# Last attention: the weighing of a head pair moved to right behind a slot's scores

## The chip, the cores and the metric

The kernel runs on one NeuronCore of a Trainium2 chip. The metric is the device time of one execution in microseconds (us), the median of several runs. The engines named below are TensorE (PE in the rows, PEld its weight loads), VectorE (DVE), ScalarE (ACT), GpSimd (POOL) and SyncE (SP). Each executes its own instructions in order and they wait for one another with semaphores.

## What is computed

The reference is a stack of four gated layers over x of 16 sequences x 256 tokens x 128 channels, all in 32 bit. Each layer normalises x, sends it through a mixer and through a feed-forward part, and adds mixer * silu(feed-forward) to x. The change touches only the mixer of the last layer, a causal attention with 16 heads of 64 channels:

```python
q = einsum('bpm,imh->bpih', x, W_Q) + b_Q      # the same for k and v
scores = einsum('bpih,bqih->bipq', q, k) / 8
scores = where(causal, scores, -100000.0)
attn = softmax(scores, axis=-1)
z = einsum('bpih,biqp->bqih', v, attn)
out = einsum('bqih,ihm->bqm', z, W_O) + b_O
```

## The kernel before, in words

The last attention is `layer3_attention`. Its unit of work is a slot m, which stands for one pair of heads of one sequence (the code calls a sequence a batch b): 16 x 8 = 128 slots, and a few more at the end in which the pipeline runs empty. There is no planner: each engine runs a loop over the slots, written out by hand, and the order of the calls in that loop is the order of its work.

On TensorE these steps exist:

- `scores(m)` (L3007, L3009): q times k of the pair, each head from its own 64 partitions (64*128 in the rows), into one of two buffers `ps`. It waits until the exponentials of slot m - 2 are done.
- `turn(m)` (L3019): six transposes of the scaled probabilities of pair m into the one buffer `pt`. It waits for GpSimd's scaling and for VectorE's copy of the previous transposes.
- `weigh(m)` (L3033, L3035): v times the turned probabilities, each head into its own 64 partitions of `pz` (128*64 in the rows).
- `job(...)`: a projection into the one buffer `px`. There are three kinds: "qk" makes q and k of one pair (L2988, L2989), "v" makes a quarter of v of a sequence (L2992), "out" applies W_O to a whole sequence (L2982, 32 matmuls). A job first waits until all jobs before it have been saved out of `px`.

`PLAN` sets which jobs go with which slot. Counted within eight slots, slots 6, 7, 0 and 1 have a qk job and then a v job; slots 2, 3 and 5 have a qk job; slot 4 has the out job of the sequence before and then a qk job. In the first sequence qk jobs crowd into slot 0, and the v jobs lie in slots 1 to 4.

TensorE's order within a slot before the change is: scores(m), first job, turn(m - 2), weigh(m - 3), remaining jobs.

The other engines follow the same slots. VectorE adds the mask to `ps` (L3173), takes the maxima (L3175, L3177), saves k of a qk job or the result of an out job out of `px` (L3120, L3122), takes the reciprocal of the sums of slot m - 1 (L3185) and copies `pt` of slot m - 2 to `turned` (L3191); in slots 3 to 17 it also has steps of the routing of the next part. Before saving k it waits for ScalarE's save of q of the same job. ScalarE saves q (L3064) and v (L3070) out of `px`, makes the exponentials (L3078, four per slot), and saves z out of `pz` (L3087). Its order is: save of the first job, exponentials of m, save of z of m - 3, save of the second job. GpSimd scales the exponentials with the reciprocals (L2963, L2964) and copies the next x (L2956). SyncE issues six loads of weights at the beginning and nothing later.

The line numbers of the loops are those of the code below.

Of the kernel before, what the change touches and what calls it, by code (L numbers as in the profile page):

```python
# [2893 lines left out]
def layer3_attention(nc, c, st, w, ready, fetch, fetched, spent, logits, gate_b, w_tok, spare):  # L2894
# [6 lines left out]
    ALL = NB * PAIRS  # L2901
# [8 lines left out]
    last = max(jobs) + 1  # L2910
# [4 lines left out]
    with ExitStack() as ctx:  # L2915
# [25 lines left out]
        with phase(nc, names, BATCH // NB, spent=spent) as (block, i, sems):  # L2941
            (bias_ready, x_ready, job_ready, job_saved, k_saved, scores_ready, masked, max_ready, exp_ready, recip_ready, prob_ready, turn_ready,
             turned_saved, z_ready, z_saved, logits_ready, chance_ready, choose_step) = sems
            SLOTS = max(ALL + 4, last)

            @block.sync
            def _(sp):
# [20 lines left out]
            @block.tensor  # L2968
            def _(pe):
                pe.wait_ge(*ready)  # L2970
                def job(what, b, n):

                    m = turn_of[what, b, n]
                    if by_act[m]:
                        pe.wait_ge(job_saved, by_act[m])
                    if by_dve[m]:
                        pe.wait_ge(k_saved, by_dve[m])
                    if what == "out":
                        pe.wait_ge(z_saved, PAIRS * (b + 1))
                        for t in range(2):  # L2980
                            for g in range(PAIRS):
                                ins = pe.matmul(px[:, t * P:(t + 1) * P], z[:, b % 2, g, t * P:(t + 1) * P], wo[:, g, :],  # L2982
                                                start=(g == 0), stop=(g == PAIRS - 1))
                    else:
                        pe.wait_ge(x_ready, b + 1)
                        x = xs[:, b % 2, :]
                    if what == "qk":
                        pe.matmul(px[:, 0:SEQ], wq[:, n, :], x, start=True, stop=True)  # L2988
                        ins = pe.matmul(px[:, SEQ:], wk[:, n, :], x, start=True, stop=True)  # L2989
                    if what == "v":  # L2990
                        t, half = n % 2, n // 2
                        ins = pe.matmul(px[:, :], x[:, t * P:(t + 1) * P], wv[:, half * HALF:(half + 1) * HALF],  # L2992
                                        start=True, stop=True)
                    ins.then_inc(job_ready, 1)

                def scores(m):

                    b, n = m // PAIRS, m % PAIRS
                    done = turn_of["qk", b, n] + 1
                    pe.wait_ge(job_saved, by_act[done])  # L3000
                    pe.wait_ge(k_saved, by_dve[done])
                    if m >= 2:
                        pe.wait_ge(exp_ready, 4 * (m - 1))
                    both = [(ps[m % 2][:, h, :], q[h * HD:(h + 1) * HD, b % 2, n, :], k[h * HD:(h + 1) * HD, b % 2, n, :])
                            for h in range(2)]
                    for out, qh, kh in both:
                        pe.matmul(out[:, 0:P], qh[:, 0:P], kh[:, 0:P], start=True, stop=True)  # L3007
                    for out, qh, kh in both:
                        ins = pe.matmul(out[:, P:3 * P], qh[:, P:], kh[:, :], start=True, stop=True)  # L3009
                    ins.then_inc(scores_ready, 1)  # L3010

                def turn(m):

                    pe.wait_ge(prob_ready, 2 * m + 2)
                    if m >= 1:
                        pe.wait_ge(turned_saved, m)
                    for h in range(2):
                        for j in range(3):
                            ins = pe.transpose(pt[:, h, j * P:(j + 1) * P], prob[:, m % 4, h, j * P:(j + 1) * P], c.ident[:, :])  # L3019
                    ins.then_inc(turn_ready, 1)  # L3020

                def weigh(m):

                    b, n = m // PAIRS, m % PAIRS
                    if n % 4 == 0:
                        pe.wait_ge(job_saved, by_act[turn_of["v", b, 2 * (n // 4) + 1] + 1])
                    if m >= 1:
                        pe.wait_ge(z_saved, m)
                    pe.wait_ge(turned_saved, m + 1)
                    both = [(pz[h * HD:(h + 1) * HD, :], slice((2 * n + h) * HD, (2 * n + h + 1) * HD), turned[:, m % 2, h, :])  # L3030
                            for h in range(2)]
                    for out, cols, pr in both:
                        pe.matmul(out[:, 0:SEQ], v[:, b % 2, 0, cols], pr[:, 0:SEQ], start=True, stop=False, skip_group_check=True)  # L3033
                    for out, cols, pr in both:
                        ins = pe.matmul(out[:, P:SEQ], v[:, b % 2, 1, cols], pr[:, SEQ:], start=False, stop=True,  # L3035
                                        skip_group_check=True)
                    ins.then_inc(z_ready, 1)

                for m in range(SLOTS):
                    now = jobs.get(m, [])  # L3040
                    if m == 0:
                        job(*now[0])
                        now = now[1:]
                    if m < ALL:
                        scores(m)
                    for j in now[0:1]:
                        job(*j)
                    if 0 <= m - 2 < ALL:
                        turn(m - 2)
                    if 0 <= m - 3 < ALL:  # L3050
                        weigh(m - 3)
                    for j in now[1:]:
                        job(*j)

            @block.scalar
            def _(act):
                load_table(act, c, ACT.Exp)
                act.wait_ge(bias_ready, 1)
                def save(what, b, n):
                    act.wait_ge(job_ready, turn_of[what, b, n] + 1)  # L3060
                    if what == "qk":
                        if b >= 2:
                            act.wait_ge(scores_ready, PAIRS * (b - 2) + n + 1)
                        act.activation(q[:, b % 2, n, :], px[:, 0:SEQ], ACT.Identity, bias=bq8[:, n:n + 1], scale=1 / 8)\  # L3064
                           .then_inc(job_saved, 1)
                    else:
                        t, half = n % 2, n // 2
                        if b >= 2:
                            act.wait_ge(z_ready, PAIRS * (b - 1))
                        act.activation(v[:, b % 2, t, half * HALF:(half + 1) * HALF], px[:, :], ACT.Copy).then_inc(job_saved, 1)  # L3070

                def exp(m):
                    act.wait_ge(max_ready, 2 * m + 2)
                    if m >= 4:
                        act.wait_ge(turn_ready, m - 3)
                    for h in range(2):
                        for t, cols in ((0, slice(0, P)), (1, slice(P, 3 * P))):
                            act.activation(prob[:, m % 4, h, cols], ps[m % 2][:, h, cols], ACT.Exp, bias=neg_max[:, m % 4, h, t:t + 1],  # L3078
                                           accum_out=total[:, m % 4, h, t:t + 1]).then_inc(exp_ready, 1)

                def save_z(g):
                    b, n = g // PAIRS, g % PAIRS
                    act.wait_ge(z_ready, g + 1)
                    if b >= 2 and n == 0:
                        act.wait_ge(job_ready, turn_of["out", b - 2, 0] + 1)

                    act.activation(z[:, b % 2, n, :], pz[:, 0:SEQ], ACT.Identity, bias=bv[:, n:n + 1]).then_inc(z_saved, 1)  # L3087

                for m in range(SLOTS):
                    now = jobs.get(m, [])  # L3090
                    if m == 0:
                        save(*now[0])
                        now = now[1:]
                    for j in now[0:1]:
                        if j[0] != "out":
                            save(*j)
                    if m < ALL:
                        exp(m)
                    if 0 <= m - 3 < ALL:
                        save_z(m - 3)  # L3100
                    for j in now[1:]:
                        if j[0] != "out":
                            save(*j)
                    if m == 4:
                        act.wait_ge(logits_ready, 1)
                        act.activation(chance[:, :, :], chance[:, :, :], ACT.Exp, scale=-1.0).then_inc(chance_ready, 1)

            @block.vector
            def _(dve):
# [53 lines left out]

                for m in range(SLOTS):
                    now = jobs.get(m, [])
# [258 lines left out]
```

## Time and profile before

| | |
|---|---|
| median of 3 runs | 2275.07 us (2269.94 to 2275.17) |
| span of the profiled execution | 2277.2 us |
| this attention, first scores to start of the next part | 1540 to 2123 us |
| granted clock, mean over the span | 0.934 |
| TensorE busy over the span | 2059.6 us (90%) |

The span is that of one execution under the profiler. It lies 2.1 us above the median of the timed runs. Busy time of TensorE counts matmuls whose ends are modelled, so distances between starts say more than durations.

### The profile page before, as it was taken

To read this page: it belongs to the slowest core of one execution; us is meant where nothing else is said; L and a number is where in the kernel's file an instruction comes from. 1 tells how busy PE (TensorE), PEld (TensorE's weight loads), DVE (VectorE), ACT (ScalarE), POOL (GpSimd) and SP (SyncE) were. 2 spreads that over 40 slices of the span, in tenths; PEclk is the share of its full clock that TensorE was granted. 3 is DMA by queue.
4 is the path that set the end of the run, shared out by engine and by line. 5 is a ranking of instruction groups with operands and counts; after the bars stand their busy time and mean duration, and the time that the engine had idled before them with its cause. 6 is when DMAs were issued, how large, how long until landed. Compare 5 with 4: busy or idle time off the path is not lost. (4 is left out here: it accounts for less than half of the span.)

```text
span 2277.2 us, 47255 instructions
## 1 busy us (share of the span) xinstructions
PE 2059.6 (90%) x18551; PEld 1392.9 (61%) x18551; DVE 1348.3 (59%) x3481; ACT 1049.2 (46%) x2520; POOL 631.5 (28%) x720
## 2 busy tenths in 40 slices
PE   4989999988879999698867897959999999999998
PEld 2546666657766677454555555655666666666565
DVE  2017777754555555456536884147877777677677
ACT  4235656642244454322234436345666666666222
POOL 3016930002210000103762015652333333333000
PEclk9989999998999999899986558988999999999999
DMA  2026030002110000241251013330000000000000
GB/s 62 19 29 29 2 39 2 2 5 65 18 55 1 1 1 1 69 140 22 39 138 39 2 28 114 48 87 25 1 1 1 1 1 1 1 1 1 6 15 19
DMA packets 118330, 64.44 MB, mean 28 GB/s; under 512 B 65848, under 2 KB 113248, under 8 KB 116960
## 3 DMA queue, kind: packets, MB, share of 16 engines
q1 hardware_dynamic: 106128, 52.37, 9.8%
q0 software_dynamic: 11264, 8.66, 2.7%
q8 instruction: 150, 2.46, 0.5%
q14 instruction: 68, 0.56, 0.1%
q10 hardware_dynamic: 720, 0.40, 0.1%
HBM read 37.54 MB, written 23.86 MB: 27 GB/s over the span
## 5 line engine op out<-in xcount | busy, mean ns | idle before, releaser
L3078 ACT ACTIVATE l_prob<-l_ps,l_neg_max 128x128 f32<-128x128 f32 (+1 forms) x512 | 208.6, 420 | 47.3 <-DVE l_neg_max L3177 42.5
L1658 ACT ACTIVATE l0a_prob<-l0a_pst 128x1024 f32<-128x1024 f32 x128 | 131.2, 1025 | 119.7 <-PE l0a_pst L1576 119.7
L2963 POOL TENSOR_TENSOR l_prob<-l_prob,l_total 128x256 f32<-128x256 f32 x128 | 78.6, 614 | 366.0 <-DVE l_total L3185 366.0
L1709 DVE TENSOR_REDUCE l0a_peak<-l0a_ps 128x4 f32<-128x1024 f32 x128 | 156.2, 1221 | 15.8 <-PE l0a_ps L1571 13.7
L1571 PE MATMUL l0a_ps<-l0a_k,l0a_q 32*128 32x256 f32 x1024 | 146.3, 405 | 3.3 <-ACT l0a_prob L1658 2.5
L680 ACT ACTIVATE l0e_hidden<-l0e_ph,l0f_b 128x512 f32<-128x512 f32 x128 | 87.9, 687 | 129.2 <-PE l0e_ph L591 129.2
L1576 PE MATMUL l0a_pst<-l0a_q,l0a_k 32*128 32x256 f32 x1024 | 145.8, 400 | 0.2 <-ACT l0a_prob L1658 0.2
L3173 DVE TENSOR_TENSOR l_ps<-l_ps,future 128x512 f32<-128x512 f32 x128 | 89.4, 699 | 93.2 <-PE l_ps L3009 93.0
L601 PEld LDWEIGHTS l0e_py<-l0f_w,l0e_hidden 128*128 128x128 f32 x1024 | 119.7, 192 | 35.0 <-ACT l0e_hidden L680 32.6
L2964 POOL TENSOR_TENSOR l_prob<-l_prob,l_total 128x512 f32<-128x512 f32 x128 | 133.2, 1041 | 0.0
L601 PE MATMUL l0e_py<-l0f_w,l0e_hidden 128*128 128x128 f32 x1024 | 129.8, 280 | 0.3 <-ACT l0e_hidden L680 0.3
L3064 ACT ACTIVATE l_q<-l_px,l_bq 128x256 f32<-128x256 f32 x128 | 60.7, 474 | 144.1 <-PE l_px L2989 144.1
L591 PE MATMUL l0e_ph<-l0f_h_ch,l0f_w 128*128 128x512 f32 x256 | 123.3, 596 | 2.9 <-ACT l0e_hidden L680 1.8
L3191 DVE COPY l_prob_t<-l_pt 128x768 f32<-128x768 f32 x128 | 119.2, 931 | 4.0 <-PE l_pt L3019 1.8
L1571 PEld LDWEIGHTS l0a_ps<-l0a_k,l0a_q 32*128 32x128 f32 x1024 | 91.5, 187 | 30.5 <-issue 22.6
L3019 PE MATMUL l_pt<-ident,l_prob 128*128 128x128 f32 x768 | 105.0, 273 | 2.9 <-POOL l_prob L2964 2.6
L3078 ACT ACTIVATION_READ_ACCUMULATOR l_prob<-l_ps,l_neg_max 128x1 f32 x512 | 104.1, 203 | 0.0
L709 DVE SCALAR_TENSOR_TENSOR l0e_acc<-l0e_py,l0e_w,l0e_acc 128x128 f32<-128x128 f32 x192 | 54.1, 344 | 83.0 <-PE l0e_py L601 82.8
L3019 PEld LDWEIGHTS l_pt<-ident,l_prob 128*128 128x128 f32 x768 | 91.1, 141 | 15.3 <-POOL l_prob L2964 4.4
L2988 PE MATMUL l_px<-l_x,l_wq 128*128 128x256 f32 x256 | 91.1, 438 | 10.1 <-issue 5.6
L1576 PEld LDWEIGHTS l0a_pst<-l0a_q,l0a_k 32*128 32x128 f32 x1024 | 89.9, 184 | 1.5 <-issue 1.2
L1285 POOL TENSOR_TENSOR gr_k_in<-gr_k_tok,gd_k_scale 128x512 f32<-128x512 f32 x8 | 8.6, 1078 | 283.3 <-ACT gr_v_tok L1177 283.2
(533 smaller groups left out, 4936.4 us busy)
## 6 DMA issues: line engine op xcount, KB each, us to landing
l_band<-zero SPq DMA_DIRECT2D x16, 272.0 KB, 7.3
x_tok<-in_x_dram SPq DMA_DIRECT2D x2, 2048.0 KB, 8.3
l2f_w<-in_L_ffn_w_dram SPq DMA_DIRECT2D x2, 2048.0 KB, 10.0
l_rows<-l_band SPq DMA_DIRECT2D x16, 256.0 KB
l1f_w<-in_L_ffn_W_dram SPq DMA_DIRECT2D x3, 1024.0 KB, 11.3
gd_tri<-gp_tri SPq DMA_DIRECT2D x8, 256.0 KB, 2.0
l0f_w<-gd_tri SPq DMA_DIRECT2D x8, 256.0 KB, 11.5
gd_tri<-l0f_w SPq DMA_DIRECT2D x8, 256.0 KB, 8.4
```

What stands on the lines that cost most here:

```text
L591: pe.matmul(ph1[u % 2][:, :], w1[:, unit, :], x, start=True, stop=True).then_inc(h1_ready, 1)
L601: ins = pe.matmul(py[x % 2][:, j, :], hidden[:, x % 2, f, j * P:(j + 1) * P], w2[:, (x % n_exp) * chunks + f, :], start=(f == 0), stop=(f ...
L1571: ins = pe.matmul(ps[m % 2][:, j, t, :], left, right, start=True, stop=True)
L1576: ins = pe.matmul(pst[:, j, t, :], left, right, start=True, stop=True)
L1658: act.activation(prob[:, (n // 2) % 2, pair, :, :].rearrange("p g t s -> p g (t s)"), pst[:, :, :, :].rearrange("p g t s -> p g (t s)"), A ...
L1709: dve.tensor_reduce(to, ps[m % 2][:, :, :, :], AX.X, ALU.max, negate=True).then_inc(max_ready, 1)
L2964: pool.tensor_tensor(far, far, total[:, m % 4, :, 1:2].to_broadcast([P, 2, 2 * P]), ALU.mult).then_inc(prob_ready, 1)
L2988: pe.matmul(px[:, 0:SEQ], wq[:, n, :], x, start=True, stop=True)
L3019: ins = pe.transpose(pt[:, h, j * P:(j + 1) * P], prob[:, m % 4, h, j * P:(j + 1) * P], c.ident[:, :])
L3078: act.activation(prob[:, m % 4, h, cols], ps[m % 2][:, h, cols], ACT.Exp, bias=neg_max[:, m % 4, h, t:t + 1], accum_out=total[:, m % 4, h, ...
L3173: dve.tensor_tensor(diag, diag, future, ALU.add).then_inc(masked, 1)
L3191: dve.tensor_copy(turned[:, n % 2, :, :], pt[:, :, 0:3 * P]).then_inc(turned_saved, 1)
```

## The change

The weighing of a pair happens one slot later, and at another place in the slot: directly behind the scores, ahead of the first job. The order on TensorE becomes scores(m), weigh(m - 4), first job, turn(m - 2), remaining jobs. ScalarE's save of z moves with it, to the beginning of its slot. The number of slots is bounded by the pipeline's depth plus one; it stays 133, since the last out job already lies in slot 132. VectorE's, GpSimd's and SyncE's loops are as before.

```diff
-            SLOTS = max(ALL + 4, last)
+            SLOTS = max(ALL + 5, last)
...
             @block.tensor
...
                     if m < ALL:
                         scores(m)
+                    if 0 <= m - 4 < ALL:
+                        weigh(m - 4)
                     for j in now[0:1]:
                         job(*j)
                     if 0 <= m - 2 < ALL:
                         turn(m - 2)
-                    if 0 <= m - 3 < ALL:
-                        weigh(m - 3)
                     for j in now[1:]:
                         job(*j)
...
             @block.scalar
...
+                    if 0 <= m - 4 < ALL:
+                        save_z(m - 4)
                     for j in now[0:1]:
                         if j[0] != "out":
                             save(*j)
                     if m < ALL:
                         exp(m)
-                    if 0 <= m - 3 < ALL:
-                        save_z(m - 3)
                     for j in now[1:]:
                         if j[0] != "out":
                             save(*j)
```

## Rows read from the trace of the kernel before

**Rows 1.** Busy time per engine in one stretch: engines' us, granted clock, DMA share.

```profile
core 0: us, PE busy (x) PEld busy (x) DVE busy (x) ACT busy (x) POOL busy (x), PEclk, DMA share, GB/s
...
1600.00:2100.00 500.00, 493.15 (x3483) 335.93 (x3481) 357.49 (x696) 316.55 (x1182) 185.82 (x239) 1.00 0.01 1
```

**Rows 2.** Timeline of TensorE over one batch: start, us, engine, line, tiles.

```profile
1819.98 0.49 PE L3007 MATMUL l_ps<-l_k,l_q 64*128 64x128 f32 x4
...
1827.88 1.12 PE L2992 MATMUL l_px<-l_wv,l_x 128*128 128x512 f32 x2
1828.94 0.49 PE L3007 MATMUL l_ps<-l_k,l_q 64*128 64x128 f32 x4
...
1837.90 0.49 PE L3007 MATMUL l_ps<-l_k,l_q 64*128 64x128 f32 x4
...
1838.76 0.70 PE L2988 MATMUL l_px<-l_x,l_wq 128*128 128x256 f32 x2
1839.30 0.59 PE L2989 MATMUL l_px<-l_x,l_wk 128*128 128x256 f32 x2
1839.73 0.82 PE L3019 MATMUL l_pt<-ident,l_prob 128*128 128x128 f32 x6
1840.48 0.65 PE L3033 MATMUL l_pz<-l_prob_t,l_v 128*64 128x256 f32 x4
...
1841.28 0.49 PE L3007 MATMUL l_ps<-l_k,l_q 64*128 64x128 f32 x4
...
1843.10 0.82 PE L3019 MATMUL l_pt<-ident,l_prob 128*128 128x128 f32 x6
...
1849.18 0.82 PE L3019 MATMUL l_pt<-ident,l_prob 128*128 128x128 f32 x6
...
1851.27 0.59 PE L2989 MATMUL l_px<-l_x,l_wk 128*128 128x256 f32 x2
1851.79 0.49 PE L3007 MATMUL l_ps<-l_k,l_q 64*128 64x128 f32 x4
...
1853.09 0.67 PE L2988 MATMUL l_px<-l_x,l_wq 128*128 128x256 f32 x2 [0.38 <-issue]
...
1855.58 0.49 PE L3007 MATMUL l_ps<-l_k,l_q 64*128 64x128 f32 x4
```

**Rows 3.** Timeline of TensorE in the first layer's attention, 32-row to 32-column blocks.

```profile
398.83 0.37 PE L1576 MATMUL l0a_pst<-l0a_q,l0a_k 32*128 32x256 f32 x1
399.14 1.07 PE L1604 MATMUL l0a_pz<-l0a_prob,l0a_v 128*32 128x256 f32 x16
```

**Rows 4.** Timeline of all engines in the third slot of the last attention.

```profile
1554.16 0.59 PE L2989 MATMUL l_px<-l_x,l_wk 128*128 128x256 f32 x2
...
1554.59 0.82 PE L3019 MATMUL l_pt<-ident,l_prob 128*128 128x128 f32 x6
1554.79 0.47 ACT L3064 ACTIVATE l_q<-l_px,l_bq 128x256 f32<-128x256 f32 x1 [1.32 <-PE l_px L2989]
...
1555.41 0.47 DVE L3120 TENSOR_SCALAR l_k<-l_px,l_bk 128x256 f32<-128x256 f32 x1
...
1555.99 1.10 PE L2992 MATMUL l_px<-l_wv,l_x 128*128 128x512 f32 x2 [0.58 <-issue]
...
1557.01 0.38 PE L3007 MATMUL l_ps<-l_k,l_q 64*128 64x128 f32 x2
```

**Rows 5.** Timelines of VectorE and of GpSimd within the batch of rows 2.

```profile
1843.33 0.68 DVE L3177 TENSOR_REDUCE l_neg_max<-l_ps 128x2 f32<-128x512 f32 x1
...
1845.62 0.70 DVE L3173 TENSOR_TENSOR l_ps<-l_ps,future 128x512 f32<-128x512 f32 x1 [0.30 <-PE l_ps L3009]
...
1849.38 0.42 DVE L3122 TENSOR_TENSOR mixer_out<-l_px,l_bo 128x256 f32<-128x256 f32 x1 [2.00 <-PE l_px L2982]
...
1841.76 1.04 POOL L2964 TENSOR_TENSOR l_prob<-l_prob,l_total 128x512 f32<-128x512 f32 x1
```

**Rows 6.** Timeline of TensorE, where slots 4 and 22 start.

```profile
1561.44 0.49 PE L3007 MATMUL l_ps<-l_k,l_q 64*128 64x128 f32 x4
...
1641.96 0.49 PE L3007 MATMUL l_ps<-l_k,l_q 64*128 64x128 f32 x4
```

## The prediction

> **What bounds the kernel now.** I read the views in this order. First the busy time by stage: in 500 us of this attention TensorE is busy 493, VectorE 357, ScalarE 317, GpSimd 186, and the granted clock is 1.00, the 2.4 GHz level [rows 1]. So the stage is TensorE's, and the question is what fills it. Second TensorE's timeline of one batch of eight slots [rows 2]. The reader is to look there at the distance from one start to the next, not at the durations, because the durations overlap. The batch takes 1855.58 - 1819.98 = 35.60 us. Its four slots with a q/k job and a v job take (1837.90 - 1819.98)/4 = 4.48 on the average (I call them v slots); a slot with a q/k job alone takes 3.38 (1837.90 to 1841.28); the slot with the output job takes 7.14 (it starts another 3.37 after 1841.28, at 1844.65, and ends at 1851.79); the one after it takes 3.79, because its q/k job starts 1.82 us after the previous q/k job's second half (1851.27 to 1853.09).
>
> **The hidden price: changes of shape.** In [rows 2] the second half of a q/k job (two passes of 256 columns) takes 0.43 us with a block of the same 128*128 shape before and behind it (1839.30 to 1839.73). The first half is the same work and takes 0.54, as it comes behind the 64-row scores. So a block that begins with a change of shape pays 0.10 more. Ahead of the scores the second half takes 0.52 (1851.27 to 1851.79), so a block that ends in a change pays 0.09 more. The weighing (128*64) streams as many columns per head as the scores, and takes 0.80 (1840.48 to 1841.28) against 0.86 (1837.90 to 1838.76); I take its beginning as 0.05. Prices of one change, end and beginning together: scores to job 0.19, transposes to weighing 0.14, weighing to scores 0.19, weighing to job 0.19, job to scores 0.19; job to transposes and back costs nothing.
>
> **The change on TensorE.** No matmul is added or removed, only the order differs, and no DMA issue, SP or GpSimd instruction moves. The 0.80 us of weighing goes from behind the transposes to ahead of the job.
> - A slot with one job: before scores | job, transposes | weighing | (three changes); after scores | weighing | job, transposes | (three). By the blocks: 0.86 + 0.80 + 0.97 + 0.75 = 3.38 both ways. Scores to weighing does not occur in this stage. The nearest rows are those of the first layer's attention, where 32-row matmuls are followed by 128*32 ones: the last step is 399.14 - 398.83 = 0.31 [rows 3], where one pass of 256 columns takes 0.21 (half of 0.43). So it ends at 0.10, and I take 0.14 in all, like transposes to weighing. From below it could be nothing, from above 0.19; over 128 slots that is -18 to +6 us round my value.
> - A slot with two jobs: before four changes (0.19 + 0.14 + 0.19 + 0.19 = 0.71), after three (0.14 + 0.19 + 0.19 = 0.52). With everything ready a v slot would take 0.86 + 0.80 + 0.97 + 0.66 + 0.96 = 4.25: six transposes without a change behind them (0.75 - 0.09) and a v job without one ahead (1.06, from 1827.88 to 1828.94, less 0.10).
>
> **The wait that comes in.** All jobs write one bank, px. The second job's first matmul waits until ScalarE has saved q and VectorE, which waits for that save, has saved k. Before, transposes and weighing (0.75 + 0.80) lie between the q/k job and the v job; after, only the transposes. The trace already holds this very order: in the third slot (1554 us) there is nothing to weigh yet, and transposes are followed at once by the v job [rows 4]. q/k's second half starts at 1554.16, ScalarE's save of q at 1554.79, VectorE's save of k at 1555.41, over at 1555.88, and the v job at 1555.99: 1.83 after 1554.16, the same distance as the 1.82 of [rows 2]. Unhindered it would be 0.43 + 0.66 = 1.09. The wait is 0.74. Then the v job takes 1.02 (1555.99 to 1557.01) rather than 0.96, since its weights were not loaded ahead. A v slot after the change: 0.86 + 0.80 + 0.97 + 1.40 (1554.59 to 1555.99) + 1.02 = 5.05, against 4.48: +0.57.
>
> Could another engine make it later or earlier? VectorE's maxima end 2.73 behind the slot's start (1843.33 + 0.68 - 1841.28 [rows 2, 5]); after the change q/k's second half starts at 0.86 + 0.80 + 0.54 = 2.20 and the k save at 2.20 + 1.25 = 3.45, so VectorE stands waiting. ScalarE's step that now comes first, the save of z, can start when the weighing ends at 1.66 and is as short as q's (0.47); q's save starts at 2.20 + 0.63 = 2.83. Both saves are bound to the job's end alone, and nothing shortens them.
>
> **What follows from the shift elsewhere.** In one-job slots the k save, the reciprocal, GpSimd's scaling and the transposes that wait for it all shift by the same 0.80; scaling now ends at 1841.76 + 1.04 = 1842.80 and the transposes start at 1843.10 [rows 2, 5], so a slack of 0.30 stays. VectorE now needs 1.31 us from the end of the maxima (1844.01) through k save, reciprocal and copy of the transposed block, until it idles 0.30 before the mask at 1845.62 [rows 5]. With the k save at 3.45 these would end at about 3.45 + 1.31 + 0.1 = 4.86 behind the slot's start, where the next mask wants to begin at 3.38 + 0.97 = 4.35 (1845.62 less the slot's start at 1844.65): 0.5 late. But the maxima then end at 2.73 + 0.5 = 3.2 of their slot and the next k save is not due before 3.45, so the lateness does not add up.
> - Slot with the output job: after its last pass (0.11 before 1849.18) VectorE saves at 1849.38 for 0.42 [rows 2, 5], plus 0.10 until TensorE: 1849.90, which is 0.72 behind the transposes' start where 0.66 would do. In place of -0.19 I take -0.06 (bounds -0.19 and 0).
> - The slot behind it: the weighing now lies between the two q/k jobs and covers the wait: 3.79 becomes 3.38, -0.41.
>
> **The sum.** v slots from slot 4 on: one in the first batch and four in each of 15: 61 x 0.57 = +34.8. Some starting waits, where VectorE also does the routing, go under in the longer slots: slots 4 to 21 take 1641.96 - 1561.44 = 80.52 [rows 6], and the steady pattern would give 9 x 4.48 + 5 x 3.38 + 2 x (7.14 + 3.79) = 79.1: -1.4. Output slots 15 x -0.06 = -0.9. The slots behind them 15 x -0.41 = -6.2. Slot 3 loses its weighing and gets the wait: -0.2. In the tail TensorE waits for others, and one more weighing fits in there: 0, at most +-1. Together +26 us. The profiled span is 2277.2, 2 us above the median of 2275.1 and inside what runs differ by; I add to the median: **2301 us**.
>
> **A rule for the change and one against it.** The rows show 0.14 to 0.19 us per change of shape [rows 2]; this mechanism by itself is the rival "switches" below. The Trainium skill, TensorEngine Tiling (Array Packing), "Key Properties", says that changing the tiling mode, not merely the tile, drains the engine; by that rule alone the change is a gain. The rows also show px emptied 1.72 us behind the start of q/k's second half (1555.88 - 1554.16 [rows 4]). The same page of the Trainium skill, "PSUM Bottleneck", warns that tiling hastens TensorE and not the emptying of PSUM; by it the change only moves the wait, and the trace agrees.
>
> **Rivals.**
> - *Switches*: the px wait is hidden after all. Then 76 slots with two jobs save 0.19 (-14.4), and the waits behind the output job go (-6.2): 2254 us, faster. For it: the prices of changes are plain in [rows 2]. Against: [rows 4] shows transposes to v job at 1.40. It decides below a wait of about 0.3 us, for which the k save would have to come 0.45 earlier, as if it did not follow q's.
> - *The loop slips too*: the 0.30 of slack behind GpSimd is eaten, and the transposes wait about 0.2 in most slots: 128 x 0.2 = +26 more, 2327 us. Against it, all its links shift alike.
> - *Nothing*: scores to weighing costs nothing (-18), and the wait is 0.15 us shorter than [rows 4] show (61 x 0.15 = -9): 2301 - 27 = 2274 us.
>
> **How the numbers follow.** Forecast 0.84, switches 0.06, slipping loop 0.07, nothing 0.03. The forecast's own bounds are 2301 - 18 and 2301 + 6 from the unseen change, and some 6 us for starts that come later than in [rows 4]; the range is 2284 to 2315. What this kernel's measurement can tell from no change is 0.3%, about 7 us: faster 0.06, same 0.03, slower 0.91.
>
> **What would show it.** Right: v slots at 5.0 to 5.1 us, an idle time of about 0.6 ahead of each L2992 group released by the k save (some 35 us in all, where now there is none), 3.38 in one-job slots, and no idle ahead of L2988. Wrong: v slots near 4.24 (switches), one-job slots over 3.5 with idle ahead of L3019 (slipping loop), or one-job slots well off 3.38 with no idle (the unseen change).

## The result and the profile after

The changed kernel takes 2304.65 us (median, 2298.46 to 2306.24) against 2272.51 us for the kernel before, run beside it: a ratio of 1.0134, 95% interval 1.011 to 1.0159. That is +30 us (25 to 36), where +26 was forecast (2301, range 2284 to 2315). Its profiled span is 2302.6 us against 2277.2.

TensorE's timeline of one sequence after the change; it answers to [rows 2].

```profile
1831.10 0.49 PE L3007 MATMUL l_ps<-l_k,l_q 64*128 64x128 f32 x4
1831.43 0.60 PE L3009 MATMUL l_ps<-l_k,l_q 64*128 64x256 f32 x4
1831.96 0.65 PE L3033 MATMUL l_pz<-l_prob_t,l_v 128*64 128x256 f32 x4
1832.44 0.39 PE L3035 MATMUL l_pz<-l_prob_t,l_v 128*64 128x128 f32 x4
1832.76 0.70 PE L2988 MATMUL l_px<-l_x,l_wq 128*128 128x256 f32 x2
1833.30 0.59 PE L2989 MATMUL l_px<-l_x,l_wk 128*128 128x256 f32 x2
1833.73 0.82 PE L3019 MATMUL l_pt<-ident,l_prob 128*128 128x128 f32 x6
1835.12 1.10 PE L2992 MATMUL l_px<-l_wv,l_x 128*128 128x512 f32 x2 [0.58 <-issue]
1836.15 0.49 PE L3007 MATMUL l_ps<-l_k,l_q 64*128 64x128 f32 x4
...
1851.29 0.49 PE L3007 MATMUL l_ps<-l_k,l_q 64*128 64x128 f32 x4
...
1854.66 0.49 PE L3007 MATMUL l_ps<-l_k,l_q 64*128 64x128 f32 x4
...
1858.03 0.49 PE L3007 MATMUL l_ps<-l_k,l_q 64*128 64x128 f32 x4
...
1863.37 0.82 PE L3019 MATMUL l_pt<-ident,l_prob 128*128 128x128 f32 x6
1864.09 0.67 PE L2988 MATMUL l_px<-l_x,l_wq 128*128 128x256 f32 x2
1864.60 0.59 PE L2989 MATMUL l_px<-l_x,l_wk 128*128 128x256 f32 x2
1865.12 0.49 PE L3007 MATMUL l_ps<-l_k,l_q 64*128 64x128 f32 x4
...
1868.49 0.49 PE L3007 MATMUL l_ps<-l_k,l_q 64*128 64x128 f32 x4
```

The v slot takes 1836.15 - 1831.10 = 5.05 us, and 1.39 of it lie between the start of the transposes and the v job (1833.73 to 1835.12). The one-job slot takes 3.37 (1851.29 to 1854.66), the slot with the output job 7.09 (1858.03 to 1865.12), the one behind it 3.37 (to 1868.49), where it was 3.79. A sequence takes 1868.49 - 1831.10 = 37.39, against 35.60 in [rows 2].

What TensorE's own instructions waited for, from 1600 to 2100 us (total, times, longest). It is the only line; in the kernel before this stretch had 5.4 us ahead of L2988 and 0.4 ahead of L2992. The view names no releaser ("issue"), but the times of the two saves below do.

```profile
PE l_px L2992 <- issue: 30.9, 53, 0.9
```

The chain in that v slot on ScalarE and VectorE: save of q, save of k, then the v job above. It answers to [rows 4].

```profile
1833.93 0.47 ACT L3064 ACTIVATE l_q<-l_px,l_bq 128x256 f32<-128x256 f32 x1 [0.58 <-PE l_px L2989]
1834.54 0.48 DVE L3120 TENSOR_SCALAR l_k<-l_px,l_bk 128x256 f32<-128x256 f32 x1 [0.30 <-ACT l_q L3064]
```

The save of k ends at 1834.54 + 0.48 = 1835.02, the v job starts at 1835.12. VectorE had nothing to do for 0.30 before it, and the releaser is ScalarE's save.

### The profile page after: what moved, and what is told of

The parts are those of the page before. It is cut to its first block and busy times, and to the rows that moved or that the text cites. A ratio compares the mean times of both kernels' runs of the same rounds, so it can differ in the third digit from the quotient of the medians.

```text
span 2302.6 us, 47255 instructions
## 1 busy us (share of the span) xinstructions
PE 2068.1 (90%) x18551; PEld 1397.4 (61%) x18551; DVE 1349.6 (59%) x3481; ACT 1056.5 (46%) x2520; POOL 631.4 (27%) x720
## 5 line engine op out<-in xcount | busy, mean ns | idle before, releaser
L3120 DVE TENSOR_SCALAR l_k<-l_px,l_bk 128x256 f32<-128x256 f32 x128 | 61.9, 483 | 76.9 <-ACT l_q L3064 76.8
L3087 ACT ACTIVATE ffn_out<-l_pz,l_bv 128x256 f32<-128x256 f32 x128 | 60.8, 475 | 98.3 <-PE l_pz L3035 98.2
L2992 PE MATMUL l_px<-l_wv,l_x 128*128 128x512 f32 x128 | 71.1, 637 | 38.1 <-issue 36.9
## 6 DMA issues: line engine op xcount, KB each, us to landing
l0f_w<-gd_tri SPq DMA_DIRECT2D x8, 256.0 KB, 12.7
```

## The experiments

Each ratio is against runs of the kernel before on the same chip. The chips differ from one experiment to another, so the ratios are to be compared and not the medians. "Sequence" is the distance between the starts of slots 62 and 70 in the trace, the eight slots of one sequence in the steady part, in us.

| kernel | sequence | less before, x 15 | ratio, 95% interval |
|---|---|---|---|
| before | 35.60 | | |
| changed | 37.39 | +27 | 1.0134 (1.011 to 1.0159) |
| v job first | 35.33 | -4 | 0.9991 (0.9969 to 1.0014) |
| TensorE's part alone | 40.72 | +77 | 1.0333 (1.0289 to 1.0376) |
| k saved later | 38.73 | +47 | 1.0217 (1.0175 to 1.0259) |
| z saved early, old order | 35.39 | -3 | 0.9984 (0.9963 to 1.0004) |
| two orders | 35.62 | 0 | 1.0013 (0.9997 to 1.0029) |
| two orders, z behind v | 35.53 | -1 | 1.0002 (0.9983 to 1.0021) |
| one more change of shape | 35.92 | +5 | 1.0059 (1.0038 to 1.0081) |
| the same, reciprocals early | 35.08 | -8 | 0.9973 (0.9954 to 0.9992) |

(The last row is the kernel with two orders and z behind v, with early reciprocals.)

**The v job ahead of the q/k job.**

```diff
+    for t in jobs:
+        if t:
+            jobs[t].sort(key=lambda job: job[0] != "v")
```

> The changed kernel, but in slots with a q/k job and a v job the v job goes first. TensorE's changes of shape per slot stay three. Theory (the wait on px decides): the second job now waits for ScalarE's one save of v (starts 0.64 behind v's last pass, 0.62 long, 0.10 to TensorE), and no longer for two saves in a row; the wait falls from 0.74 to about 0.26 us, v slots from 5.05 to 4.57, 61 of them: 29 us less than the changed kernel, about 2275, level with the kernel before. Rival (the new order costs elsewhere, px is innocent): v slots stay at 5.05 and the time at 2304.

Measured 2273.33 us, ratio 0.9991 where the changed kernel has 1.0134: its whole loss is gone (a sequence is 2.06 us shorter, 31 us in 15; 29 was expected). A v slot of it, TensorE and ScalarE (three lines are inserted above, so numbers are 3 higher: L2995 is the v job, L3022 the transposes, L2991 and L2992 the q/k job, L3073 the save of v):

```profile
1849.92 1.13 PE L2995 MATMUL l_px<-l_wv,l_x 128*128 128x512 f32 x2
1850.88 0.82 PE L3022 MATMUL l_pt<-ident,l_prob 128*128 128x128 f32 x6
1851.08 0.60 ACT L3073 ACTIVATE l_v<-l_px 128x512 f32<-128x512 f32 x1 [0.57 <-PE l_px L2995]
1851.73 0.70 PE L2991 MATMUL l_px<-l_x,l_wq 128*128 128x256 f32 x2
```

The second job starts 0.85 behind the transposes instead of 1.39, right behind ScalarE's save. The slot takes 4.53. It has three changes of shape as the changed kernel has, and the weighing stands where the changed kernel has it, so the loss is the wait for px and not the weighing's place by itself. The saves of q and k now lie behind the slot's other work on ScalarE and VectorE too; scores and weighing of the next slot cover them.

**TensorE's part of the change alone.**

```diff
-                    if 0 <= m - 4 < ALL:
-                        save_z(m - 4)
                     for j in now[0:1]:
...
                     if m < ALL:
                         exp(m)
+                    if 0 <= m - 4 < ALL:
+                        save_z(m - 4)
```

> The changed kernel with ScalarE's save of z back at its old place, behind the exponentials; TensorE's order stays the new one. Theory: z of a pair is then saved about 5.4 us behind its slot's start, the next weighing wants pz at 3.37 + 0.86 = 4.23, so each slot behind a one-job slot (slots 2, 3 and 5 of eight) waits 1.3 us ahead of L3033, and these slots go from 3.37 to 4.67; v slots at 5.05 cover it. 45 such slots: +58 us, about 2362. Rival (the place of z's save is free, as ScalarE is only half busy): same as the changed kernel, 2304.

Measured 2350.59 us, ratio 1.0333. The weighing waits for ScalarE, which is nearly half idle (busy 267 of 500 us) but has z's save behind four exponentials:

```profile
1804.52 0.49 ACT L3087 ACTIVATE ffn_out<-l_pz,l_bv 128x256 f32<-128x256 f32 x1
1805.07 0.65 PE L3033 MATMUL l_pz<-l_prob_t,l_v 128*64 128x256 f32 x4 [1.02 <-ACT ffn_out L3087]
```

The places were as expected (slots 3, 4 and 6 of eight), the size a little less: 4.47, 8.23 and 6.14 in place of 3.37, 7.09 and 5.05, so 1.1 each and not 1.3, and 2351 in place of 2362. ScalarE's half of the diff is therefore needed, not decoration.

**The save of k made later.**

```diff
+                        if b and n < 4:
+                            dve.tensor_reduce(dummy[:, 4 * b + n:4 * b + n + 1], px[:, SEQ:], AX.X, ALU.max)
                         dve.tensor_scalar(k[:, b % 2, n, :], px[:, SEQ:], ...).then_inc(k_saved, 1)
```

> The changed kernel with one more VectorE reduction of 256 columns out of px ahead of the save of k in the 60 slots of sequences 1 to 15 that have a v job too; its result is not used. Theory (the serial saves of q and k set the v job): VectorE's start-to-start for such a reduction is 0.34 us, all of it goes to the wait, v slots 5.05 to 5.39: +20 us, about 2325. Rival (TensorE's v job waits for something else, its weights or ScalarE): the reduction falls into VectorE's idle time and costs under 3 us.

Measured 2324.56 us, ratio 1.0217. VectorE and the v job (line numbers are 1 to 3 higher):

```profile
1855.12 0.42 DVE L3122 TENSOR_REDUCE l_dummy<-l_px 128x1 f32<-128x256 f32 x1 [0.71 <-ACT l_q L3065]
1855.46 0.47 DVE L3123 TENSOR_SCALAR l_k<-l_px,l_bk 128x256 f32<-128x256 f32 x1
1856.03 1.10 PE L2993 MATMUL l_px<-l_wv,l_x 128*128 128x512 f32 x2 [0.91 <-issue]
```

The reduction delays the save by 0.34, and TensorE's idle time goes from 0.58 to 0.91: v slots take 5.38 instead of 5.05. The v job follows the save of k one for one: 19 us more than the changed kernel by the two ratios, where 20 were expected.

**ScalarE's part alone, TensorE's order as before.**

```diff
+                    if 0 <= m - 4 < ALL:
+                        save_z(m - 4)
                     for j in now[0:1]:
...
                     if m < ALL:
                         exp(m)
-                    if 0 <= m - 3 < ALL:
-                        save_z(m - 3)
```

> The kernel before with TensorE's order untouched; only ScalarE's save of z goes to the beginning of the next slot. Theory: in the kernel before every second v slot takes 4.53 in place of 4.43, because z's save stands ahead of v's and px is released 0.1 us late for the next q/k job. With z out of the way these fall to 4.43: 30 x 0.1 = 3 us less than before, about 2270. Rival (the 4.53 is TensorE's own): same as before within 1 us. If z came too late for the weighing it would show as idle time ahead of L3033.

Measured 2272.29 us, ratio 0.9984 (0.9963 to 1.0004). The runs alone don't settle 3 us, the trace does: all v slots take 4.43, as these three starts show, where every second one took 4.53.

```profile
1814.08 0.49 PE L3007 MATMUL l_ps<-l_k,l_q 64*128 64x128 f32 x4
...
1818.51 0.49 PE L3007 MATMUL l_ps<-l_k,l_q 64*128 64x128 f32 x4
...
1822.94 0.49 PE L3007 MATMUL l_ps<-l_k,l_q 64*128 64x128 f32 x4
```

**One more change of shape, cover untouched.**

```diff
+                    if 0 <= m - 3 < ALL:
+                        weigh(m - 3)
                     if 0 <= m - 2 < ALL:
                         turn(m - 2)
-                    if 0 <= m - 3 < ALL:
-                        weigh(m - 3)
```

> The kernel before with the weighing ahead of the transposes instead of behind them, both still between the first and the second job. The cover of px is the same 1.5 us. In one-job slots the changes of shape go from three to four (scores, job, weighing, transposes, scores); in slots with two jobs they stay four. Theory (a change costs 0.19 us by itself): slots 2, 3 and 5 of eight get 0.19 longer, v slots keep their length: 45 x 0.19 = 9 us more than before, about 2281. Rival (the prices read from the starts belong to the matmuls and not to the change): same as before.

Measured 2284.8 us, ratio 1.0059 (1.0038 to 1.0081). A one-job slot of it:

```profile
1842.60 0.49 PE L3007 MATMUL l_ps<-l_k,l_q 64*128 64x128 f32 x4
...
1843.46 0.70 PE L2988 MATMUL l_px<-l_x,l_wq 128*128 128x256 f32 x2
1843.99 0.59 PE L2989 MATMUL l_px<-l_x,l_wk 128*128 128x256 f32 x2
1844.52 0.65 PE L3033 MATMUL l_pz<-l_prob_t,l_v 128*64 128x256 f32 x4
1845.00 0.39 PE L3035 MATMUL l_pz<-l_prob_t,l_v 128*64 128x128 f32 x4
1845.32 0.87 PE L3019 MATMUL l_pt<-ident,l_prob 128*128 128x128 f32 x6
1846.12 0.49 PE L3007 MATMUL l_ps<-l_k,l_q 64*128 64x128 f32 x4
```

The slot takes 3.52 and not 3.37, with no idle time: the fourth change costs 0.15, not 0.19. The transposes take 0.80 between two changes against 0.75 with one [rows 2], so their beginning costs 0.05, half of a projection's 0.10. V slots became 0.05 shorter in half of the cases (4.38), for the same reason; the steady slots' sum gives +5 us, and the runs +9 to +18. The trace shows 1.8 us more at the end: from the last scores to the next part it takes 17.13 us and not 15.35, as the weighing, now ahead of the transposes, waits there for the saves of z and for VectorE's copies (1.1 to 1.2 us each time). Slots 4 to 126 grew by 5.2 us in all. Slots 0 to 3 took another 2.8 us, at the lower clock, as in the changed kernel (see below). So a change has a price of its own, and the rival is out; what the runs show beyond these 7 us stays open.

A v slot of the same run shows the v job behind the transposes with no wait between them:

```profile
1823.96 0.87 PE L3019 MATMUL l_pt<-ident,l_prob 128*128 128x128 f32 x6
1824.67 1.02 PE L2992 MATMUL l_px<-l_wv,l_x 128*128 128x512 f32 x2
1825.63 0.49 PE L3007 MATMUL l_ps<-l_k,l_q 64*128 64x128 f32 x4
```

**Two orders: the new one only where no v job follows.**

```diff
+                    late = any(j[0] == "v" for j in now)
-                    if 0 <= m - 4 < ALL:
+                    if 0 <= m - 4 < ALL and not late:
                         weigh(m - 4)
...
                         turn(m - 2)
+                    if 0 <= m - 4 < ALL and late:
+                        weigh(m - 4)
```

(ScalarE's save of z likewise: first in its slot, or behind the exponentials. The second kernel, "z behind v", also has ScalarE save v before z in those v slots that another v slot follows.)

> The changed kernel with two orders: in slots without a v job the new one, in slots with a v job the weighing (and z's save) behind the transposes as before, so that it lies between the q/k job and the v job again. Theory (px wait loses, everything else of the change gains): v slots return to 4.43 to 4.54, the slot of the output job stays at 7.09 and the one behind it at 3.37, instead of 7.14 and 3.79; per sequence 0.47 less than before: 7 us less than before, about 2267. Rival (the mixed order brings a new wait for z or for the weighing's input): one-job slots over 3.5, no gain against before.

> As the kernel with two orders, and in the v slots that another v slot follows ScalarE saves v before z. Theory: the 4.53 of every second v slot becomes 4.43 as in the run with z's save moved; 34.9 us per sequence instead of 35.6 before: 10 us less than before, about 2263. Rival (z's save is then late for the next weighing): idle time ahead of L3033, no gain over the kernel with two orders.

Measured 2274.25 us (ratio 1.0013) and 2269.56 us (ratio 1.0002): no gain, the forecast of 7 and 10 us failed. The saved parts are there (7.09 and 3.37 in slots 4 and 5, 4.43 in v slots of the second kernel), but the first of four v slots takes 5.03. Both rivals expected no gain, but from waits at other places (one-job slots, the weighing), and these did not come. From the second kernel, the start of that slot's projections, GpSimd's scaling and the transposes:

```profile
1810.29 0.70 PE L2988 MATMUL l_px<-l_x,l_wq 128*128 128x256 f32 x2
...
1810.71 1.04 POOL L2964 TENSOR_TENSOR l_prob<-l_prob,l_total 128x512 f32<-128x512 f32 x1
1810.82 0.59 PE L2989 MATMUL l_px<-l_x,l_wk 128*128 128x256 f32 x2
...
1811.80 0.87 PE L3019 MATMUL l_pt<-ident,l_prob 128*128 128x128 f32 x6 [0.39 <-POOL l_prob L2964]
```

Without the weighing ahead of them the transposes come 0.80 earlier in this slot, while the scaling still follows the previous slot's late save of k. The slack of 0.30 behind GpSimd [rows 2, 5] does not cover it. The next run tests this reading.

**The reciprocals ahead of the save of k.**

```diff
+                    late = any(j[0] == "v" for j in now)
+                    if 1 <= m <= ALL and not late:
+                        ...
+                        dve.reciprocal(sums, sums).then_inc(recip_ready, 1)
                     for j in now[0:1]:
                         save(*j)
-                    if 1 <= m <= ALL:
+                    if 1 <= m <= ALL and late:
```

> As the kernel with two orders and z's save moved, and in slots without a v job VectorE takes the reciprocals ahead of the save of k instead of behind it. Theory (in that kernel the first of four v slots takes 5.03 because its transposes come 0.8 us earlier in the slot, while GpSimd's scaling of that pair ends where it did): the scaling then ends about 1.0 us earlier, the transposes do not wait, that slot falls to 4.43, a sequence to 34.9 us against 35.6 before, 15 sequences: 10 us less than before, about 2263. Rival (the slot waits for its q/k job's px, not for the scaling): the slot stays at 5.03 and the time at that of before.

Measured 2267.82 us against 2275.49 for the kernel before, ratio 0.9973 (0.9954 to 0.9992): 6 us faster (2 to 10), where 10 were expected. It is the only version whose interval excludes "no change" on the fast side; that of "z saved early" overlaps it. The slot falls to 4.59, not to 4.43:

```profile
1813.33 0.49 PE L3007 MATMUL l_ps<-l_k,l_q 64*128 64x128 f32 x4
...
1815.15 0.82 PE L3019 MATMUL l_pt<-ident,l_prob 128*128 128x128 f32 x6
1815.90 0.65 PE L3033 MATMUL l_pz<-l_prob_t,l_v 128*64 128x256 f32 x4
...
1816.90 1.10 PE L2992 MATMUL l_px<-l_wv,l_x 128*128 128x512 f32 x2
1817.92 0.49 PE L3007 MATMUL l_ps<-l_k,l_q 64*128 64x128 f32 x4
```

The wait ahead of the transposes is gone (0.75 to the weighing, as in [rows 2]). What is left over 4.43 is ahead of the v job, 1.00 behind the weighing's start instead of 0.80. The same slot on ScalarE and VectorE (L3067 is the save of q, L3186 the second maxima, L3129 the save of k):

```profile
1815.36 0.47 ACT L3067 ACTIVATE l_q<-l_px,l_bq 128x256 f32<-128x256 f32 x1 [0.49 <-PE l_px L2989]
1815.72 0.68 DVE L3186 TENSOR_REDUCE l_neg_max<-l_ps 128x2 f32<-128x512 f32 x1
1816.32 0.47 DVE L3129 TENSOR_SCALAR l_k<-l_px,l_bk 128x256 f32<-128x256 f32 x1
```

The save of q is over at 1815.83, and VectorE could follow at 1815.97 (0.61 behind its start, as elsewhere). It starts at 1816.32 without idle time, straight behind the maxima, and ends at 1816.79, 0.11 ahead of the v job. So here late maxima hold the save of k; no run removes them.

## Why the prediction was right

- *The wait.* The term that decides was read from a place in the trace that already had the new order [rows 4]. It gave 1.40 from transposes to v job and 5.05 for the slot; the trace after has 1.39 and 5.05. That the wait follows the two saves in a row was argued then and is shown now: one save in place of two takes the loss away (v job first), 0.34 more on VectorE comes out as 0.33 more on TensorE (k saved later).
- *Scores to weighing.* The prediction's largest unknown, -18 to +6 us. One-job slots stayed at 3.37, so my 0.14 holds: the scores' second part takes 0.53 before it (1831.43 to 1831.96) and the weighing begins as it does behind the transposes (0.48 from 1831.96 to 1832.44, as 1822.55 to 1823.03 in the kernel before).
- *What it gives back.* Slot of the output job 7.09 (forecast 7.08), the one behind it 3.37 (3.38). For the first the prediction's rows gave only 0.06 of wait, which leaves -0.13 and not its -0.06; the trace has 0.73 behind the transposes' start, and the q/k job's first half then takes 0.51 where it takes 0.43 without a wait (one more change of shape). So part of that agreement is luck.
- *The slipping loop.* It does not slip: there is no idle time ahead of the transposes in the list of waits above, and GpSimd's scaling still ends 0.31 ahead of them in a one-job slot (1856.98 to 1857.29).
- *The rival "switches".* Its mechanism is real (0.15 for the change that was added, 0.19 by the prediction's count for the one that the v slots save) but worth a quarter of the wait of 0.73 in each v slot.
- *What was mis-sized.* From first to last scores the stage takes 2133.40 - 1536.24 = 597.16 us against 2107.97 - 1540.31 = 567.66 before: +29.5, where my sum to there gives +26. The steady part comes out (13 sequences x 1.79 = 23.3, forecast 1.81 each). The starting part does not. Slots 4 to 21 grew by 3.6 and not by 2.8 us: of the -1.4 for starting waits only 0.6 came true, because VectorE's routing steps still lie in front of its mask and its saves, and now delay the v job directly. Slot 6 took 5.72 us, because VectorE's routing step (L3146) ran until the mask, and the save of k followed the maxima without idle time, although that of q was over at 1571.72:

```profile
1570.26 0.57 DVE L3146 TENSOR_SCALAR l2f_w<-l2f_w 128x192 f32<-128x192 f32 x1
1571.94 0.68 DVE L3177 TENSOR_REDUCE l_neg_max<-l_ps 128x2 f32<-128x512 f32 x1
1572.54 0.47 DVE L3120 TENSOR_SCALAR l_k<-l_px,l_bk 128x256 f32<-128x256 f32 x1
1573.12 1.10 PE L2992 MATMUL l_px<-l_wv,l_x 128*128 128x512 f32 x2 [1.25 <-issue]
```

  And slots 0 to 3 took 2.7 us more, which I had at -0.2. Slot 3 is 0.18 shorter, as forecast; slots 1 and 2 took 12.7 us instead of 9.9. There the granted clock was at the lower level (1.2 GHz) longer in this profiled execution. TensorE's share of busy time and clock, kernel after and kernel before in the same stretch:

```profile
1550.00:1555.00 5.00, 4.75 (x19) 3.42 (x20) 2.54 (x6) 2.00 (x7) 0.17 (x1) 0.60 0.00 0
```

```profile
1550.00:1555.00 5.00, 3.80 (x20) 2.12 (x20) 2.40 (x7) 2.89 (x11) 1.61 (x2) 0.99 0.01 3
```

  It is no effect of the change: the first slots before any weighing are alike in both, and of the other kernels with untouched first slots some show it (two orders with z behind v, one more change of shape: 12.7 us too) and some do not (8.9 to 9.8). Why it comes in some executions is open. Without slots 1 and 2 the stage grew by 26.7 us, close to the 26 of the sum. The span differs by 25.4 only, as the parts ahead of this stage took 4.1 us less in the profiled execution after; the change does not touch them.

## What to carry to other kernels

Before moving a block, list what waits it covers: a block between two users of one single buffer can hide a wait of up to its own length (here 0.80 of weighing hid 0.73), even on an engine that is 98% busy, and that can outweigh a real saving in the order. Look in the trace's first and last slots for a place where the pipeline is not yet full; it often already shows the order that is proposed, with the price. When only some slots can afford the new order, mixing the two shifts the blocks against the other engines at the seam, and the slack there must be checked by itself.

## What the runs showed of the hardware

- A change of a matmul's shape on TensorE costs 0.09 to 0.10 us at the end of the block before it: 0.52 against 0.43 for the second half of a q/k job [rows 2], 1.06 [rows 2] against 0.96 for the v job (v job first), 0.80 against 0.71 for the transposes (one more change of shape). At the beginning of the block behind it the kinds differ: 0.10 to 0.11 for projections (v job 1.06 [rows 2] against 0.95 to 0.96 in one more change of shape, q/k's first half 0.54 against 0.43) and 0.05 for transposes (0.80 against 0.75). No run has scores or weighing behind a block of their own shape, so the prediction's 0.10 and 0.05 for them are inferred from 0.86 and 0.80 for as many columns. The half price for transposes was new to me.
- A v job behind a wait takes 0.06 to 0.08 us more than one that follows at once (1.02 to 1.03 in the changed kernel against 0.95 to 0.96 in one more change of shape, 1824.67 to 1825.63), although both come behind the transposes and ahead of the scores.
